# Diagonal banks of the row maxima: copied by ScalarE, masked by GpSimd, reduced for two heads at once; plain banks read in place

## What is computed

```python
q = to_heads(q) * d ** (-0.5)
k = to_heads(k)
v = to_heads(v)
sim = jnp.einsum('bhqd,bhkd->bhqk', q, k)
causal_mask = jnp.triu(jnp.ones((n, n), dtype=bool), k=1)
neg = -jnp.finfo(sim.dtype).max
sim = jnp.where(causal_mask, neg, sim)
attn = jax.nn.softmax(sim, axis=-1)
out = jnp.einsum('bhqk,bhkd->bhqd', attn, v)
```

## Time and profile before

| | |
|---|---|
| median of 3 runs | 2284.18 us (2284.12 to 2285.5) |
| the profiled execution: span, first to last instruction | 2282.9 us |
| TensorE, VectorE, ScalarE, GpSimd busy | 2258.2, 1739.9, 1630.2, 201.5 us |
| granted TensorE clock, mean | 0.997 |
| attention stage | to about 1636 us |

### The profile page before, as it was taken

The page is one execution under the profiler, slowest core; times in us unless marked ns, Lnnn a source line. Parts: engine busy times, 40 slices in busy tenths (PEclk is TensorE's granted clock), DMA queues, the critical chain, the costliest instruction groups (busy, mean ns, idle before and its releaser), DMA issues. The chain is left out here.

```text
span 2282.9 us, 40342 instructions
## 1 busy us (share of the span) xinstructions
PE 2258.2 (99%) x15338; PEld 1396.3 (61%) x15338; DVE 1739.9 (76%) x3748; ACT 1630.2 (71%) x3087; POOL 201.5 (9%) x237
## 2 busy tenths in 40 slices
PE   8999999999999999999999999999999999999998
PEld 5555555555555556555555555554588888888887
DVE  8898999888889897888989898996435445544543
ACT  4677888889999898889989899999723333432332
POOL 3211100011000102000010201001100000000000
PEclk9999999999999999999999999999999999999999
DMA  3110001100000200000020000205410000000000
GB/s 102 32 26 15 6 20 40 38 20 20 20 20 1 59 20 20 20 20 19 1 56 20 20 20 20 77 1 168 152 42 15 5 19 19 10 10 19 15 5 20
DMA packets 72292, 70.17 MB, mean 31 GB/s; under 512 B 41632, under 2 KB 51744, under 8 KB 70688
## 3 DMA queue, kind: packets, MB, share of 16 engines
q1 hardware_dynamic: 67392, 56.03, 9.3%
q0 software_dynamic: 4704, 11.53, 1.7%
HBM read 28.20 MB, written 4.19 MB: 14 GB/s over the span
## 5 line engine op out<-in xcount | busy, mean ns | idle before, releaser
L723 ACT ACTIVATE PR<-bank 128x512 f32<-128x512 f32 (+1 forms) x2176 | 1094.0, 592 | 71.9 <-PE bank L1071 67.7
L813 DVE TENSOR_REDUCE pm<-bank 128x1 f32<-128x512 f32 x1422 | 920.9, 684 | 131.6 <-PE bank L1045 112.6
L1088 PE MATMUL bank<-PR,V 128*17 128x512 f32 (+3 forms) x4608 | 553.2, 562 | 0.3 <-POOL PR L621 0.3
L1486 PE MATMUL bank<-e_hid,e_h_sb 128*128 128x512 f32 x2048 | 466.1, 389 | 0.0
L1066 PE MATMUL bank<-MR,ones 64*128 64x512 f32 (+3 forms) x2304 | 458.5, 384 | 0.8 <-DVE pm L813 0.2
L1486 PEld LDWEIGHTS bank<-e_hid,e_h_sb 128*128 128x128 f32 x2048 | 383.9, 188 | 81.1 <-DVE e_hid L1356 1.5
L1308 ACT ACTIVATE e_tmp<-bank,scales 128x512 f32<-128x512 f32 x128 | 88.3, 690 | 322.8 <-PE bank L1486 322.7
L1066 PEld LDWEIGHTS bank<-MR,ones 64*128 64x128 f32 x2304 | 234.3, 185 | 77.7 <-ACT PR L723 41.9
L816 DVE CUSTOM_DVE_ANT_0 bank<-bank,below 128x256 f32<-128x256 f32 (+3 forms) x512 | 240.0, 514 | 33.0 <-PE bank L1045 31.9
L708 ACT ACTIVATE mx_sb<-bank 128x512 f32<-128x512 f32 x370 | 221.6, 599 | 60.2 <-PE bank L1045 54.4
L808 DVE TENSOR_REDUCE pm<-mx_sb 128x1 f32<-128x512 f32 x370 | 250.3, 676 | 1.0 <-ACT mx_sb L708 0.8
(11 more groups left out here) (138 smaller groups left out, 1723.4 us busy)
## 6 DMA issues: line engine op xcount, KB each, us to landing
xnT<-in_h_dram SPq DMA_DIRECT2D x8, 1024.0 KB, 4.9
KA<-qk_hi SPq DMA_DIRECT2D x88, 64.0 KB, 2.2
KA<-qk_lo SPq DMA_DIRECT2D x88, 64.0 KB, 2.2
QX<-qk_hi SPq DMA_DIRECT2D x80, 64.0 KB, 2.2
QX<-qk_lo SPq DMA_DIRECT2D x80, 64.0 KB, 2.2
xres<-in_x_dram SPq DMA_DIRECT2D x8, 512.0 KB, 8.3
e_h_sb<-in_h_dram POOLq DMA_DIRECT2D x2, 2048.0 KB, 10.8
e_h_sb<-in_h_dram POOLq DMA_DIRECT2D x1, 4096.0 KB, 23.7
```

Of the source, the lines that this page charges most:

```text
L723: act.activation(PR[:, s % NPB, h, off:QB], ring_bank("score", s, h)[:, off:QB], ACT.Exp).then_inc(exp_done, 1)
L813: dve.reduce_max(pm[:, B % 2, i, a, p, 1 + c:2 + c], bank[:, :], AX.X).then_inc(mx_done, 1)
L1088: last = pe.matmul(ACC[32 * h:32 * h + VW, q:QB], V[:, v_tile(B, tile), GH * (B // NJ % 2) + h, :], PR[:, s % NPB, h, at:at + QB - q], sta ...
L1486: last = pe.matmul(RING[(4 + n) % NR][:, :], w[:, c, P * o:P * (o + 1)], hid[:, (T + layer) % 2, part, c, :], start=(c == 0 and part == 0) ...
```

## The change

- In `maxima_of` a diagonal unit comes first of its queries and heads, where it came last.
- Diagonal units stand only behind the product (`early` takes plain units alone), and first there.
- ScalarE copies both banks of every diagonal unit to a relay buffer of 4 x 512 columns, 128 to 512 columns each, side by side (`relay`, `copy_of`). A copy waits until what it overwrites has been reduced (`former_copy`).
- GpSimd masks the last 128 columns of both halves in the copy by one `affine_select` (`cut_maxima`).
- VectorE reduces both heads in one instruction (`triangle_maximum`, the new operation `tri`), which stands two units behind the unit itself (`DEFER`), or at the block's end.
- Plain units are no longer relayed (`FULL_RELAYS` is False).
- The mask `below` is gone, and the warm-up of TensorE has 4 x 5 matmuls of 128 columns in place of 5 of 512.

```diff
+RELAY = 4 * QB
+DEFER = 2
+FULL_RELAYS = False
 def maxima_of(B):
+    chunks = [B % NJ] + list(range(B % NJ))
-    return [(i, c, p) for i in range(TI) for p in range(2) for c in range(B % NJ + 1)]
+    return [(i, c, p) for i in range(TI) for p in range(2) for c in chunks]
...
-            self.ops += units[:half]
+            half = (len(per_step[s]) + 1) // 2
+            early = [item for item in per_step[s] if not diagonal(*item)][:half]
+            self.units(early)
...
-            self.ops += units[half:] + turns.get(s, []) + last.get(s, [])
+            rest = [item for item in per_step[s] if item not in early]
+            self.units(sorted(rest, key=lambda item: not diagonal(*item)))
+            self.ops += turns.get(s, []) + last.get(s, [])
...
+    def units(self, items):
+        for item in items:
+            self.ops.append(("unit",) + item)
+            self.cut = [(held, age + 1) for held, age in self.cut]
+            if diagonal(*item):
+                self.cut.append((item, 0))
+            self.left[item[0]] -= 1
+            done = item[0] if self.left[item[0]] == 0 else None
+            for held, age in list(self.cut):
+                if age >= DEFER or held[0] == done:
+                    self.ops.append(("tri",) + held)
+                    self.cut.remove((held, age))
+            if done is not None:
+                self.ops.append(("rowmax", done))
...
+            def cut_maxima(B, n):
+                pool.wait_ge(mx_copied, PLAN.copied(B, n, 1))
+                corners = copy_of(B, n)
+                corners = corners[:, :, corners.shape[2] - P:corners.shape[2]]
+                pool.affine_select(out=corners, in_=corners, compare_op=ALU.is_ge, fill=MASK, base=0,
+                                   pattern=[[0, 2], [-1, P]], channel_multiplier=1).then_inc(mx_cut, 1)
...
-                act.activation(mx_sb[:, k % NRB, :], ring_bank("unit", B, n, 0)[:, :], ACT.Copy).then_inc(mx_copied, 1)
+                for a in range(copy_of(B, n).shape[1]):
+                    act.wait_ge(mx_ready, 2 * PLAN.index[B, n] + a + 1)
+                    if former and a == 0:
+                        act.wait_ge(mx_done, former)
+                    copy = copy_of(B, n)[:, a, :]
+                    act.activation(copy, ring_bank("unit", B, n, a)[:, 0:copy.shape[1]], ACT.Copy).then_inc(mx_copied, 1)
...
-                    dve.tensor_tensor_reduce(out=own, in0=own, in1=below[:, QB - P * (i + 1):QB], scale=1.0,
-                                             scalar=-3.0e38, op0=ALU.add, op1=ALU.max,
-                                             accum_out=pm[:, B % 2, i, a, p, 0:1]).then_inc(mx_done, 1)
+            def triangle_maximum(B, n):
+                dve.wait_ge(mx_cut, triangles[B, n])
+                dve.tensor_reduce(pm[:, B % 2, i, :, p, 0], copy_of(B, n), axis=AX.X, op=ALU.max).then_inc(mx_done, 1)
...
             def warm():
-                pe.wait_ge(consts, 3)
                 for _ in range(WARM):
-                    pe.matmul(ring_bank("norm", 0, 0)[:, :], ident[:, :], below[:, :], start=True, stop=True)
+                    for i in range(TI):
+                        pe.matmul(ring_bank("norm", 0, 0)[:, P * i:P * (i + 1)], ident[:, :], ident[:, :], start=True,
+                                  stop=True)
```

148 lines of the change are left out of this document (88 added, 60 removed).

## The result

2375.85 us median of four runs (2372.74 to 2377.18) against 2284.84 before: ratio 1.0397, 95% interval 1.0382 to 1.0412. The change makes the kernel 91 us slower; the forecast was 26 us slower, in a range that ended at 2328. The direction held and the size did not; the nearest rival, the lag that adds up, stood at 2337.

The account below looks back on a forecast made before the run. TensorE was taken to set the pace, losing time waiting for banks. Handovers 12.5, crowded places 9.3 and intro 3.9 sum to +25.7 us on 2282.9: 2308.6, so 2310 us as median, 1.1% slower; range 2275 to 2328.

Parts of the forecast that it names:

- the lag that adds up: Rival: after each 1.14 us reduction score matmuls also wait for VectorE's banks, 0.5 us in about 40 places; 2337 us, chance 0.15.
- TensorE's waits for banks decide, and VectorE's relief is worth nothing: Attention steps: TensorE sets the pace and loses time waiting for banks; VectorE's 45 us less work gains nothing.
- the first rival: VectorE is the bound and its relief comes through: 2258 us, or 2270 with a third given back; chance 0.15.
- The handover prices: Per attention step: 0.54 us for a single exponent wait, 0.38 with two early units, 0.08 for a VectorE-freed bank.
- The handover of banks: Attention steps 0 to 509: changes in which engine frees TensorE's banks cost +12.5 us together, between +5 and +30.
- +88 x 0.08: Steps 31 to 509: VectorE frees the late unit's bank in 155 steps instead of 67, +7.0 us.
- Its two banks come free by ScalarE within 1.1 us, so this alone costs nothing: A 512-column diagonal behind the product delays the next exponents by 0.5 us, but priced at nothing.
- The reduction stands two units behind its copy ... nothing: GpSimd's masks: copy and mask need 1.5 us, the reduction comes some 2.6 us later, so no cost.
- Crowded places, +9.3: Steps 103, 239 and 375, where diagonals of two blocks meet: ScalarE becomes the bound, +3.1 us each, 5 to 18 in all.
- its 1.4: Crowded places: half of three 2.5 us copy, mask, reduction chains less ScalarE's idle time, 1.4 us each.
- Intro, +3.9 - 1.3: Intro: block 0 and 1 maxima +2.7 and warm-up +1.2, together +3.9 us; bank handovers in steps 0 to 30, -1.3.
- steps of 2.67 and 3.1 us: Sign in the profile after: ordinary steps 2.67 us with plain late unit, 3.1 two steps behind a wide reduction, about 47.

Follow-up runs that it names:

- e_unmasked: Kernel before with a plain maximum in place of VectorE's masked one in all 512 diagonal banks; 2281.9 us, ratio 0.9988.
- e_place_only: Kernel before with only the new places of diagonal units; plain banks relayed, diagonal banks masked in place by VectorE; 2312.4 us, ratio 1.0124.
- e_no_copies: Changed kernel's unit order with plain relays off, but diagonal banks masked and reduced in place by VectorE as in the kernel before; 2333.0 us, ratio 1.0213.
- e_relays_off: Kernel before with no plain bank relayed, nothing else touched; 2324.3 us, ratio 1.0174.
- e_half: Kernel before with one of three units in a step before the product, where it was two; 2291.0 us, ratio 1.0028.
- e_mixed: Changed kernel with diagonal banks of blocks with B % NJ below 2 done in place by VectorE, relay buffer 3 x 512 columns; 2348.1 us, ratio 1.0282.
- e_no_mask: Changed kernel without GpSimd's masks of the copies, VectorE waiting for ScalarE's copy alone; 2355.1 us, ratio 1.0307.

## Why the prediction was right and wrong

- *TensorE's waits for banks decide, and VectorE's relief is worth nothing*: right, very nearly. 44 us of work went from VectorE, e_unmasked shows the price of such work (2.7 us for 23.5), and the first rival is out. The rule of the Trainium skill (SBUF — State Buffer, Who interferes with whom) that a tensor_reduce is not disturbed by GpSimd agrees with the traces: the plain reductions are at 684 ns with 256 masks more, as in the earlier trace rows.
- *The handover prices*: right for places alone. The bank table of e_place_only has, in steps without projections or block changes, 38 more single waits, 20 steps fewer with two early units and 49 more handovers by VectorE: 38 x 0.54 - 20 x 0.38 + 49 x 0.08 = +17, and its ordinary stretches lost 18.1. I worked this out after the run; before it I expected next to nothing.
- *The handover of banks, "the term that decides"*: this step failed, in its prices and not in its counts. +13.8 us of the sum are ordinary stretches, and they measured +43.9. The kinds of step shifted about as the bank table said, but each price was measured in the kernel before and taken over unchanged. In the changed kernel a step that waits for its own exponent takes 3.35 us and not 3.12, one with two early units 3.32 and not 3.07, one whose bank VectorE frees 2.79 and not 2.66 (table above: 25 of the 30 us missing). Two runs part the cause. With relays off in the new places (e_no_copies against e_place_only) 143 steps pass to VectorE's handover at 0.10 each, 14.3 us, and 64 with two early units, which "+88 x 0.08" left out, lose 6.8; less single waits, together 19.1 where the sum had 7.0. With the copies and two-head reductions on top (the changed kernel against e_no_copies) 122 handovers by VectorE lose 15.8, 27 steps that come to wait for their own exponent 17.2 (3.35 us each, where single waits took 3.10 in both runs without copies) and the 64 with two early units 6.9, while 121 steps whose bank is no longer freed by VectorE's last reduction, or by an exponent of their own, gain 36.9.
- *"Its two banks come free by ScalarE within 1.1 us, so this alone costs nothing"*: not shown. The treatment as a whole costs the ordinary stretches a net 6.7 us with relays off and 10.7 with relays on (28.8 - 18.1). The masks have no part in it (+44.5 without them); copies and two-head reductions were not run apart.
- *"The reduction stands two units behind its copy ... nothing"* (GpSimd): false where the copies crowd. Leaving out the masks gave 17 to 21 us. The estimate of 1.5 us for copy and mask had no term for GpSimd's other work, which stands before the mask there (L673, L657).
- *Crowded places, +9.3*: measured +30.0. I made ScalarE's work the bound (35 us) with half a chain on top. ScalarE was not full: it waited 1.40 us for VectorE and 1.23 for TensorE, which stood for copies (1.12) and reductions (0.81). The places alone are 9.4, which the sum didn't have at all, so that the likeness to its 9.3 is chance; the treatment, that is the serial chain with the slow clock behind it, is 20.5. The bound from above (each chain waited out, 18) was too low as well, since it had neither the cost of the places nor the clock. It doesn't follow from its own terms either: its 1.4 is half of 7.5 (three chains) less 2.35, and 3 x (1.7 + 7.5 - 2.35) is 20.6.
- *Intro, +3.9 - 1.3*: measured +14.3. The chain in block 0 was found and was 2.2 us short (33.99 for 31.8), of which some 1.4 are GpSimd's other work before the masks, as estimated above; the eight steps and more after it, where blocks 1 to 3 have the densest diagonals and the clock falls again (0.85 for 0.94), I priced by the handover table alone.
- *The lag adds up* (third rival, 2337) had the right sign, and its mechanism can be seen: at 732.73 us, behind a reduction of 1.21, a weight load of the score waits 0.16 for VectorE, and every kind of step that waits got dearer in the ordinary stretches. It had +30 for the handovers, +18 for the crowded places and +5 for the intro; measured are 52.8 (steps 0 to 30 included), 30.0 and 5.4. The Trainium skill's rule for gaps that repeat (Perfetto Trace Analysis, Optimization Strategy) fits one part, the 0.1 us in the steps where VectorE's handover takes the place of ScalarE's (e_relays_off).
- *What was not thought of*: the granted clock, up to 19 us. Of the crowded places' 20.5 us at most 12 are the slow matmuls, by the clock of the three places; no run separates them from the waits.
- *A reading*: the prediction has ScalarE's copy overlap its neighbours on either side by 0.07 us. The earlier trace rows shows the exponents from 629.68 to 631.75 and the next ones at 632.28, and the copy between them, at 631.75 for 0.60, overlaps only the latter. ScalarE's records thus leave no gap in the ordinary step. That it is not the bound is shown by e_relays_off, which takes its copies away and is slower.

In the terms of the sum: the crowded places were 21 us too low, the ordinary stretches 30, the intro and steps 0 to 30 12; that is 63 of the 65 missing, and the rest is mostly the profiled execution being the fastest of its four. Of the signs that the prediction named, VectorE's busy time (44 us less), steps 239 to 249 over 36 us and the missing plain copies came; ScalarE without gaps at the crowded places and steps of 2.67 and 3.1 us didn't.

## What to carry to other kernels

An engine's busy share says little about what a link on it costs: the mask was priced by 9% busy, and without it the kernel was some 20 us faster, because copy, mask and reduction stand in a row with a buffer that holds few of them. Before a chain over three engines takes the place of one instruction, look for the places where its units come back to back. Add up copy, mask, reduction, the wait for the buffer and whatever else the engines in the chain have in hand there, not over the whole run.

In a ring that is one buffer short, count for every step who frees each buffer and when, and price every step in which the freeing engine changes. A price that was measured in the kernel before holds only while the rest of the step stays as it was: here every kind of waiting step became 0.13 to 0.25 us dearer. A better handover in one step (e_half) can take the buffer from the next. And the cost of a part depends on its company: the new places cost 28 us alone and gave 45 back beside the new treatment.

## What the runs showed of the hardware

In each of the three crowded places of the changed kernel TensorE stood still twice, for 1.1 and 0.8 us, and behind both gaps the granted clock was at 1.2 GHz for several microseconds. The same steps of e_mixed have no gap over 0.35 us and show 1.00 throughout. A gap that long is not needed for it, though: e_no_mask has none over 0.5 us there, and the clock still fell once in each place (means of the places 0.92, 0.96 and 0.92). The windows of e_mixed from step 239 (at 810.87 us there) to beyond step 243 (826.73):

```profile
810.00:815.00 5.00, 5.00 (x37) 2.56 (x35) 2.68 (x9) 3.33 (x6) 1.97 (x3) 1.00 0.08 18
815.00:820.00 5.00, 4.94 (x37) 3.51 (x41) 4.44 (x24) 3.20 (x9) 2.06 (x3) 1.00 0.43 105
820.00:825.00 5.00, 5.00 (x46) 2.33 (x40) 3.61 (x11) 3.63 (x7) 0.84 (x2) 1.00 0.41 101
825.00:830.00 5.00, 4.69 (x32) 2.56 (x34) 4.68 (x16) 2.26 (x5) 0.00 (x0) 1.00 0.04 8
```

GpSimd's mask of 256 elements takes 0.41 us (0.68 for 512, 1.10 for 1024), and the plain reductions beside such masks kept their 684 ns. The longest negation is 1.10 us where it was 0.91; it stands at 61.58 us, inside a mask of 1024 elements on `PR` (61.55, 1.10 us) as before, and not beside a new one:

```profile
L901 DVE TENSOR_SCALAR mneg<-rowmax x32: 165/172/1096, 34.2 to 1647.6; 128x16 fp32r<-128x16 f32 x32
```
